# A Mamba block with a memory-routed FFN on one core: the warm-up units replaced by a prologue written out per engine

## What is computed

```
xs  = pixel_shuffle(layernorm_over_channels(x), 2)     # 128 channels, 48 x 48 tokens
seq = concat(global_token, xs as a sequence)           # 2305 tokens for each of 4 images
u, z = split(seq @ in_proj_w.T)                        # 256 inner channels each
u   = silu(causal depthwise conv of 4 taps over u + conv_b)
dt, B, C = split(u @ x_proj_w.T)                       # ranks 8, 16, 16
dt  = softplus(dt @ dt_proj_w.T + dt_proj_b)
h_t = exp(dt_t * A) * h_(t-1) + (dt_t * u_t) * B_t     # 16 states per channel, along the tokens
y   = (sum over states of h_t * C_t + u * D) * silu(z)
x   = x + pixel_unshuffle(y @ out_proj_w.T)
x   = x + ffn(layernorm(x))                            # a routed mix of memory tokens overwrites 128 tokens
```

## Time and profile before

| | us |
|---|---|
| median of three runs | 1269.06 (1267.61 to 1270.39) |
| the profiled execution | 1268.71 |
| its span | 1266.9 |
| busy: POOL, DVE, PE, ACT | 1107.5, 1100.3, 1084.2, 875.3 |

### The profile page before, as it was taken

One profiled execution on the slowest core, in us unless ns is written; L12 is line 12 of the kernel. 1 busy time (PEld: TensorE's weight loads), 2 busy tenths in 40 slices (PEclk: granted clock), 3 DMA queues, 4 the chain that ended last, 5 costly groups with the idle time before them and its releaser, 6 DMA issues.

```text
span 1266.9 us, 13315 instructions
## 1 busy us (share of the span) xinstructions
PE 1084.2 (86%) x3786; PEld 629.6 (50%) x3786; DVE 1100.3 (87%) x1269; ACT 875.3 (69%) x1628; POOL 1107.5 (87%) x753
## 2 busy tenths in 40 slices
PE   6669988888998998888998888899898889979887
PEld 4335545554554554545555544555455445545444
DVE  1299999999989999999899999899999999998672
ACT  2577776776767767767768768767767767667552
POOL 4189899999898999998999999998999999987662
PEclk8699999999999999999999999999999999989799
DMA  6221231322222212212212222222212213223461
GB/s 164 77 77 63 95 100 59 106 90 70 100 71 93 102 58 106 102 58 106 100 59 106 84 76 91 92 83 81 102 62 103 97 62 111 93 77 120 145 209 37
DMA packets 64539, 116.80 MB, mean 92 GB/s; under 512 B 34218, under 2 KB 47954, under 8 KB 64466
## 3 DMA queue, kind: packets, MB, share of 16 engines
q1 hardware_dynamic: 64466, 115.96, 27.1%
HBM read 108.47 MB, written 7.47 MB: 92 GB/s over the span
## 4 chain that ended last, share of the span: by engine, by line
PE 32%; ACT 24%; POOL 16%; DVE 15%; issue 12%; POOLq 0%; DMA 0%; DVEq 0%; SPq 0%; ACTq 0%
PE Yp L738 12%; DVE SCAN L1002 11%; POOL SCAN L427 7%; ACT DA L504 6%; PE PP L889 6%; POOL SCAN L439 3%; DVE SCAN L966 3%; PE PP L871 3%; PE PP L854 2%; PE PP L821 2%; PE PP L767 2%; ACT GATES L610 2%; ACT GATES L601 2%; ACT GATES L604 2%; ACT GATES L608 2%
## 5 line engine op out<-in xcount | busy, mean ns | idle before, releaser
L1002 DVE TENSOR_TENSOR_SCAN SCAN<-DA,CAR,SCAN 128x384 f32<-128x384 f32 x768 | 728.1, 997 | 52.8 <-ACT DA L504 33.2
L427 POOL TENSOR_TENSOR SCAN<-SCAN,CS 128x768 f32<-128x768 f32 x384 | 692.2, 1820 | 47.7 <-DVE SCAN L1002 43.4
L738 PE MATMUL Yp<-SCAN,IDENT 128*128 128x384 f32 x1536 | 589.3, 510 | 64.2 <-POOL SCAN L427 56.0
L504 ACT ACTIVATE DA<-UDT,A 128x384 f32<-128x384 f32 x768 | 431.7, 577 | 260.7 <-DVE SCAN L1002 257.7
L738 PEld LDWEIGHTS Yp<-SCAN,IDENT 128*128 128x128 f32 x1536 | 288.4, 197 | 262.2 <-POOL SCAN L427 102.5
L966 DVE TENSOR_TENSOR SCAN<-UDT,BB 128x768 f32<-128x768 f32 x288 | 268.0, 931 | 8.3 <-PE BB L720 8.2
L439 POOL TENSOR_TENSOR SCAN<-UDT,BS 128x768 f32<-128x768 f32 x96 | 175.0, 1823 | 0.0
L889 PE MATMUL PP<-XN,WT 128*128 128x384 f32 x384 | 140.5, 501 | 5.0 <-ACT GZ L635 5.0
L889 PEld LDWEIGHTS PP<-XN,WT 128*128 128x128 f32 x384 | 72.8, 194 | 64.3 <-issue 20.8
L720 PE MATMUL BB<-PT,SEL 96*128 96x384 bf16 x288 | 97.5, 339 | 3.0 <-DVE SCAN L966 3.0
L455 POOL TENSOR_TENSOR UDT<-UDT 128x768 f32<-128x768 f32 x24 | 43.6, 1815 | 49.2 <-DVE UDT L1083 49.2
(11 more groups left out here) (172 smaller groups left out, 1160.2 us busy)
## 6 DMA issues: line engine op xcount, KB each, us to landing
CS<-bc_rows SPq DMA_DIRECT2D x96, 768.0 KB, 4.0
BS<-bc_rows SPq DMA_DIRECT2D x24, 768.0 KB, 6.0
out<-XN SPq DMA_DIRECT2D x32, 192.0 KB, 2.4
X<-in_x SPq DMA_DIRECT2D x24, 192.0 KB, 3.5
X<-in_L_ffn_memory_tokens SPq DMA_DIRECT2D x16, 256.0 KB, 3.1
XN<-in_L_ffn_memory_tokens SPq DMA_DIRECT2D x16, 256.0 KB, 3.1
bc_rows<-XDT SPq DMA_DIRECT2D x24, 48.0 KB, 1.5
X<-in_L_ffn_memory_router SPq DMA_DIRECT2D x1, 512.0 KB, 3.7
```

The source lines that it names most:

```text
L427: pool.tensor_tensor(M[:, n1 % MRING], HB[:, n1 % HRING], over_halves(CS[:, n1 % CRING]), ALU.mult).then_inc(m_ready, 1)
L504: act.activation(DA[:, h, 0:T], DT[:, par, h], ACT.Exp, scale=A[:, h, n:n + 1])\
L738: last = pe.matmul(Yp[:, h, 0:T], IDENT[:, :], M[:, n3 % MRING, h], start=n3 == 0, stop=n3 == NS - 1)
L1002: dve.tensor_tensor_scan(HB[:, s % HRING, h], DA[:, h, 0:T], HB[:, s % HRING, h], CAR[:, ds(J * NS * HALVES + s * HALVES + h, 1)], ALU.mul ...
```

## The change

The three warm-up units go, and each engine gets a prologue() that is written out in straight lines; the loop starts at unit 0. In the prologue:

- SEL is cleared and filled at GpSimd's start, ahead of its wait for the weights, and no longer between the norm of unit 1 and the gate of unit 0.
- The transposed weights go to DA, not to PP; the projection of unit 0 goes to Yp's second bank (XQ), the global token's results to Yp's first bank (ST0), the mean and variance of units 1 and 2 to BB's two banks. Only the conv halves use PP, and DA holds the step-size projection.
- Unit 0 is convolved right after the weights, ahead of the norm of unit 1.
- The gate of unit 0 runs in halves: exp, clamp, Ln, exp and product of half 0 go while half 1 is convolved, and each half of the projection follows its product.
- XDT is copied ahead of PART, and the step-size projection comes ahead of the remainders. Abs is taken in halves.
- The Relu and the affine step (L595, L615) of unit 0 go; VectorE does all three products of the softplus, and dt u, which GpSimd did.
- The global token's small steps lie between the large ones; its last part (VectorE) comes after dt u.
- Unit 2's variance and the second half of unit 1's convolution come between the first and the second spread of B. ScalarE no longer waits for the starting states ahead of the first decays.

In the loop only the semaphore counts of Relu and the affine step change (by one, since unit 0 no longer gives them).

```diff
-            unit(-3, 1, main=False, front=False, back=False, conv=False)
-            if before_conv:
-                before_conv()
-            unit(-2, 0, main=False, front=False, back=False)
-            if before_front:
-                before_front()
-            unit(-1, 1, main=False, back=False)
...
 @block.gpsimd
+            pool.memset(SEL[:, :, :], 0.0).then_inc(zeroed, 1)
+            for part in range(PARTS):
+                pool.wait_ge(zeroed, 3 + part)
+                pool.affine_select(out=SEL[:, :, :], in_=SEL[:, :, :], compare_op=ALU.not_equal, fill=1.0,
+                                   base=-part * BC, pattern=[[-1, NS], [0, P]], channel_multiplier=1)\
+                    .then_inc(zeroed if part < PARTS - 1 else sel_ready, 1)
             pool.wait_ge(w_loaded, 16 * N_WLOADS)
...
+            normalize(0)
+            for h in range(HALVES):
+                pool.wait_ge(gate_exp, h + 1)
+                pool.tensor_scalar(SG[:, h], SG[:, h], EXP_LIMIT, 0.0, ALU.min, ALU.max)\
+                    .then_inc(clamped if h else gate_clamped, 1)
+            normalize(1)
+            normalize(2)
...
 @block.tensor
+            def prologue():
+                mean(0, STAT)
+                variance(0, STAT)
+                pe.wait_ge(ident_ready, 1)
+                pe.wait_ge(set_dve, 1)
+                for h in range(HALVES):
+                    for k in range(TAPS):
+                        last = pe.transpose(Yp[:, h, k * P:(k + 1) * P], WSC[:, h * TAPS + k], IDENT[:, :])
...
+                pe.wait_ge(set_act, 3)
+                pe.wait_ge(xn_ready, 1)
+                conv_half(0, 0)
+                conv_half(0, 1)
+                pe.wait_ge(set_act, 4)
+                pe.wait_ge(half_u, 1)
+                pe.matmul(XQ[0:XROWS, :], XPT[:, 0], U[:, 0, 0], start=True, stop=False)
...
+                mean(1, BB[:, 0, 0:TOK])
+                pe.wait_ge(u_ready, 1)
+                pe.matmul(XQ[0:XROWS, :], XPT[:, 1], U[:, 0, 1], start=False, stop=True).then_inc(xp_ready, 1)
+                pe.wait_ge(xdt_ready, 1)
+                for h in range(HALVES):
+                    pe.matmul(DA[:, h, 0:T], DTW[DTROW:XROWS + 1, h], XDT[DTROW:XROWS + 1, :],
+                              start=True, stop=True, tile_position=(DTROW, 0)).then_inc(dtp_ready if h else half_dt, 1)
+                variance(1, BB[:, 0, 0:TOK])
...
+                mean(2, BB[:, 1, 0:TOK])
...
+                pe.wait_ge(xn_ready, 2)
+                conv_half(1, 0)
             def first_main():
                 pe.wait_ge(parts_ready, 1)
                 pe.wait_ge(sel_ready, 1)
+                pe.wait_ge(ln_done, 2)
                 spread_b(0, 0, 0)
+                variance(2, BB[:, 1, 0:TOK])
+                conv_half(1, 1)
+                pe.wait_ge(ln_done, 3)
                 spread_b(0, 0, 1)
...
 @block.scalar
...
+                act.wait_ge(conv_ready, 2)
+                act.activation(SG[:, 1], PP[:, 1, 0:T], ACT.Exp, bias=NCB[:, 1:2], scale=-1.0).then_inc(gate_exp, 1)
+                act.wait_ge(clamped, 1)
+                act.activation(SG[:, 1], SG[:, 1], ACT.Ln, bias=1.0).then_inc(sg_chain, 2)
+                act.wait_ge(sg_chain, 2)
+                act.activation(SG[:, 1], SG[:, 1], ACT.Exp, scale=-1.0).then_inc(sg_ready, 1)
...
+                square(1)
+                act.wait_ge(xp_ready, 1)
+                act.activation(XDT[XROW0:XROWS, :], XQ[XROW0:XROWS, :], ACT.Copy).then_inc(xdt_ready, 1)
+                act.activation(PART[:, :], XQ[0:DTROW, :], ACT.Copy).then_inc(hi_ready, 1)
...
             def first_main():
                 act.wait_ge(dt_ready, 1)
-                act.wait_ge(car_saved, 4 * BATCH)
...
 @block.vector
+            def prologue():
+                center(0, STAT)
+                dve.wait_ge(w_loaded, 16 * N_WLOADS)
...
+                dve.wait_ge(gate_ready, 1)
+                dve.scalar_tensor_tensor(out=U[:, 0, 0], in0=PP[:, 0, 0:T], scalar=CB_[:, 0:1], in1=SG[:, 0],
+                                         op0=ALU.add, op1=ALU.mult).then_inc(half_u, 1)
...
+                dve.wait_ge(m1_done, 2)
+                dve.scalar_tensor_tensor(out=DT[:, 0], in0=DA[:, :, 0:T], scalar=0.0, in1=SE[:, :, :],
+                                         op0=ALU.max, op1=ALU.subtract).then_inc(dt_ready, 1)
+                dve.wait_ge(dt_ready, 1)
+                dve.tensor_tensor(DTU[:, 0], DT[:, 0], U[:, 0], ALU.mult).then_inc(dtu_ready, 1)
```

More of the change, by code:

```diff
@@ L401, in _, with normalize @@
                 pool.tensor_copy(XN[:, b * SLOT + HIST - 1:b * SLOT + HIST], TKC).then_inc(const_ready, 1)
-            def selectors():
-                pool.memset(SEL[:, :, :], 0.0).then_inc(zeroed, 1)
-                for part in range(PARTS):
-                    pool.wait_ge(zeroed, 3 + part)
-                    pool.affine_select(out=SEL[:, :, :], in_=SEL[:, :, :], compare_op=ALU.not_equal, fill=1.0,
-                                       base=-part * BC, pattern=[[-1, NS], [0, P]], channel_multiplier=1)\
-                        .then_inc(zeroed if part < PARTS - 1 else sel_ready, 1)
+            def normalize(g):
+                pool.wait_ge(rstd_ready, g + 1)
+                for r1 in range(2):
+                    pool.tensor_tensor(seq_rows(unit_seq(g), r1), by_row_parity(XC[:, :, :], r1),
+                                       by_row_parity(over_q(RSTD[:, :]), r1), ALU.mult).then_inc(xn_part, 1)
+                pool.wait_ge(xn_part, 2 * (g + 1))
+                pool.tensor_copy(XN[:, ds((g + BATCH) * SLOT, HIST)],
+                                 XN[:, ds(g * SLOT + T, HIST)]).then_inc(xn_ready, 1)
             def step(J, par, s, main, front, back, prev, conv, norm):
@@ L460, in step @@
                 if norm and s == 15:
[L462 to L470 removed]
+                    normalize(g)
+            normalize(0)
[5 more added lines that the diff above has]
+            normalize(2)
+            run_units(pool, step)
         @block.scalar
@@ L915, in step, with mean, variance @@
                     last.then_inc(dtp_ready, 1)
+            def mean(g, stat):
+                pe.wait_ge(x_first[g], 16)
+                for q in range(Q):
+                    last = pe.matmul(stat, MEANW[:, :], unit_x(g)[:, q], start=q == 0, stop=q == Q - 1)
+                last.then_inc(mean_ready, 1)
+            def variance(g, stat):
+                pe.wait_ge(sq_ready, g + 1)
+                for q in range(Q):
+                    last = pe.matmul(stat, MEANW[:, :], SQ[:, q], start=q == 0, stop=q == Q - 1)
+                last.then_inc(var_ready, 1)
@@ L932, in _ @@
             last.then_inc(set_dve, 1)
-            def weights():
-                dve.wait_ge(w_loaded, 16 * N_WLOADS)
-                dve.wait_ge(ident_ready, 1)
-                for h in range(HALVES):
-                    dve.tensor_scalar(DD[:, h], IDENT[:, :], DV[:, h:h + 1], None, ALU.mult)
-                dve.memset(LESS[:, :, :], 0.0).then_inc(less_set, 1)
-                dve.wait_ge(less_set, 1)
-                for part in range(1, PARTS):
-                    rows = slice(part * BC, (part + 1) * BC)
-                    for step in range(part):
-                        last = dve.tensor_scalar(LESS[rows, step], IDENT[rows, 0:DTROW], -1.0, None, ALU.mult)
-                last.then_inc(less_set, 1)
             X0v = X[:, 0:BATCH * T].rearrange("p (b q t) -> p q b t", b=BATCH, q=Q)[:, :, :, 0]
@@ L1087, in first_main @@
                 drive(0, 0, 0, 0)
-            run_units(dve, step, before_conv=weights, first_main=first_main)
+            prologue()
+            run_units(dve, step, first_main=first_main)
 _NAMES = ["x", "L0_conv_global_token", "L0_conv_in_proj_w", "L0_conv_conv_w", "L0_conv_conv_b",
```

300 lines of the change are left out of this document (180 added, 120 removed).

## The result

| | before | after |
|---|---|---|
| median of the runs beside each other | 1269.72 (1267.61 to 1270.60) | 1251.12 (1250.23 to 1255.59) |
| the profiled execution, its span | 1268.71, 1266.9 | 1250.23, 1248.5 |
| first scan starts | 64.47 | 45.72 |
| from the first scan to the end of the span | 1202.4 | 1202.8 |

The ratio of after to before is 0.9861, with a 95% interval from 0.9840 to 0.9881. The forecast was 1253.0 in a range from 1246 to 1261.

The account below looks back on a forecast made before the run. Bound: a 64.5 us start-up of engines waiting for each other, then a loop filled by VectorE, GpSimd and TensorE. 7.2 + 3.1 + 2.5 + 4.2 + 4.2 - 5.0 = 16.2; median 1269.06 less 16 gives 1253.0 us, range 1246 to 1261.

Parts of the forecast that it names:

- SEL at GpSimd's start: Opening: VectorE's eight conv-weight scalings take turns with GpSimd's selects, so unit 0's centring starts 5.0 us later, at 12.1.
- rival 1: Opening: selects do not hold up the weight scalings; first scan at 43.3, time 1248 us; chance 0.22.
- The convolution's start: Unit 0, TensorE: with the weights in DA the convolution can follow the last transpose, 7.2 us less.
- The convolution's clock: Unit 0's convolution takes 5.2 us at full clock, 3.1 less than before, with 10.2 as the other end.
- rival 2: Prologue: TensorE's clock stays low, 7.5 us less gain, time 1260.5 us; chance 0.21.
- The gate: Unit 0, convolution's end to second product's end: in halves 2.8 us instead of 5.3, 2.5 less.
- The projection: Unit 0, second product's end to end of XDT's copy: 1.7 us instead of 5.9, 4.2 less.
- From Abs to the first scan: Last stretch of the start-up: 17.3 us, taken between 16.8 and 18.5, against 17.25 before, so no gain.
- Moving SEL off the chain is worth 0.8: Before unit 0's gate clamp: selects and clearing take 8.2 us, but moving them gains 0.8, the convolution being late right behind.
- At no cost: Prologue: B and C rows arrive in time, decays go under the wait for starting states, changed counts cost nothing.
- Rival 3: Before the first scan: the B rows or a mis-ordered wait give back 16 us, time 1269; chance 0.04.
- Rival 4: Loop: a mean clock near 0.88 costs 0.8 us per unit, 17 us in all, time 1270 to 1274; chance 0.03.

Follow-up runs that it names:

- e5: Changed kernel with unit 0's gate in one piece (both exps, one clamp, one Ln, one exp, then both products): 1258.88 us, ratio 0.9914 to the kernel before.
- e9: Changed kernel with the edits of e1, e7 and e8 together: 1245.42 us, ratio 0.9807 to the kernel before.
- e1: Changed kernel with SEL's first select behind GpSimd's token copies, the other two behind unit 0's norm product: 1247.06 us, ratio 0.9820 to the kernel before.
- e3: Kernel before with only SEL's clearing and selects moved to GpSimd's start: 1271.73 us, ratio 1.0016 to the kernel before.
- e4: Changed kernel with unit 1's norm put back ahead of unit 0's convolution on every engine, still in the new banks: 1258.32 us, ratio 0.9904 to the kernel before.
- r3: Changed kernel run again as it is, in the third group: 1251.11 us, ratio 0.9858 to the kernel before.
- r0: Changed kernel run again as it is, in the first group: 1252.20 us, ratio 0.9860 to the kernel before.
- r2: Repeat of e1, selects in GpSimd's gaps of the changed kernel, in the third group: 1248.09 us, ratio 0.9829 to the kernel before.
- e8: e1 with VectorE's first product with B placed behind dt u, inside the token's chain: 1248.78 us, ratio 0.9839 to the kernel before.
- e7: Changed kernel with three extra float32 matmuls, results unread, ahead of TensorE's waits for XPT, u and XDT: 1249.91 us, ratio 0.9842 to the kernel before.
- e2: Kernel before with only the selects for SEL moved one stage earlier, ahead of unit 1's norm: 1269.12 us, ratio 0.9992 to the kernel before.

## Why the forecast was right, step by step

**The whole.** The forecast said that what the first scan gains, the end gains. 18.75 us at the first scan and 18.4 at the end: right. The 1202 us behind it held within 0.4. In the other kernels they lay between 1202.1 (e5) and 1208.3 (e9), so this holds to a few microseconds for a single execution, and the coincidence of 0.4 is partly luck. The experiments undid three parts of the change, one at a time: the place of the selects, the order of unit 1's norm and the halves of the gate. What the rest is worth (the projection behind its halves, the step-size projection ahead of the remainders, the softplus on VectorE) is read from the timelines alone.

**SEL at GpSimd's start.** Forecast 5.0 us for the centring, by turns. Measured 4.12 (7.07 to 11.19). The two engines do take turns, but the eight were through sooner, at 11.27 and not 12.1: with three held up out of eight, one went before the first select and two passed for each select, the one held up and a short one behind it, so that one was left over at the end, not four or five. L1010 was the right row to choose, and e1 and e3 show that the selects are the cause and that rival 1 is wrong. The trace agrees with the page "SBUF — State Buffer" of the Trainium skill, section Who interferes with whom, and now for a select too: 2039 ns at the longest where 279 is the median without one.

**The convolution's start.** Forecast 7.2 us for the banks. Putting unit 1's norm back in e4 takes about 5 of them; the rest is the time in which TensorE waited for PP to be emptied (2.11 us idle ahead of L849), which no run put back. The last transpose (L978) ends at 17.35 and L959's record begins at 17.18, so nothing lies between them. The start was 1.9 us earlier than forecast: 0.9 from the centring, 0.2 from that overlap, and 0.9 between centring and the last transpose, 6.16 us (11.19 to 17.35) against 7.02 before (7.07 to 14.09 in the earlier trace rows), since TensorE's clock rose earlier among the transposes. In r3, where it rose 2 us later than in the first profile, the same stretch took 7.0 again and the start was 17.96, so this 0.9 is luck of the execution. The forecast had left what the clock may give back in the range.

**The convolution's clock.** Forecast 5.2 against 10.2. Measured 5.33 in the first profile, r0, r3, e1, r2, e8 and e9. But e4, e5 and e7 took 6.6 to 7.2, since there the clock rose only within it. So the choice was right as the likeliest, and rival 2 was a live case for a part of it. Its bound of 10.2 leaves out the tail that 5.2 has in it; it should have been 10.5, and no profile came near it.

**The gate.** 3.04 for 2.8: the half clamp was mis-sized at 0.45 and took 0.51, the Ln, the second exp and the product took 0.02 to 0.05 more each, and the handovers 0.3 for 0.2. The gain is 2.3 us, from 5.3, and the halves are not all of it. e5 shows 4.5 for the undivided gate at that place, so halving is worth 1.5. With only the selects moved (e2) the same stretch of the kernel before takes 4.6 (29.91 to 34.55), so 0.7 is the clamp that no longer waits for them, and 0.1 is left for the order around it.

**The projection.** 1.52 for 1.7. ScalarE was in square(1) as said, but the projection's own end (26.49) was only 0.1 before square's (26.56), so that it was not about 1.0 late but in time.

**The step size.** 2.13 for 2.1.

**From Abs to the first scan.** 16.52 for 17.3, and 14.95 in r3. Three VectorE operations at 0.91 are 2.7, not the 2.9 of the sum, which they happened to take (38.77 to 41.72). The sum's form was right: VectorE's list ended last (L1219, 43.64 + 0.25) and TensorE's second spread (43.38 + 0.33) just ahead of it, though the clock had fallen. Its size was not. At the full clock ScalarE's list from Abs to the last of the softplus took 8.0 us (from 29.97 in r3 to 37.96, where L1192 starts, which waits for the last of them), not 9.6: the rows of such a view overlap, and I had added them up whole with handovers on top. In the first profile the wait of 1.53 at L718 filled the gap, and so the forecast looked better than it was. The whole error at the first scan, 48.3 - 45.72 = 2.6 us, is 1.9 for the convolution's start and 0.8 for this part, less 0.2 for the steps in between, and 0.1 of rounding.

**Moving SEL off the chain is worth 0.8.** e2 gained 0.7 in the median, which can't be told from nothing, and in its profile 0.66 at the clamp and 0.4 at the first scan, counted from the convolution's end.

**At no cost.** Right for the rows of B and C: the DMA share is 0.88 from 30 to 38 us, 0.06 from 38 to 40 and 0.00 behind, ahead of the scan. That the x tiles of the kernel before were all but through by 26 us does not follow from the share of 0.85 that the forecast cites; they were, as the share from 26 to 28 us is 0.00.

**The rivals.** Rival 1 fell with L1047's longest record, and with e1 and e3. Rival 2 (7.5 us less gain) did not come, but its mechanism is real: a fall of the clock behind the convolution took 1.6 us in one execution of the same program and nothing in another. Rival 3: no wait was mis-ordered. Rival 4: from the first scan on the mean clock was 0.95 (0.96 before), and the stretch cost the same as before.

## What to carry to other kernels

Before setup work is moved to an engine's empty stretch, look at what the other engine of the pair VectorE and GpSimd does there: eight instructions of 0.28 us took 6.9 beside three selects of 2.1, and with the selects in later gaps they took 1.66 again. A piece on the chain of waits is worth only what lies between it and the next thing that is late (8.2 us on it, 0.7 in the time), so name that next thing before you price the piece. And where an order leaves TensorE idle ahead of a chain of small matmuls, put that chain at the slow clock into the range: the gate in one piece cost 6.7 us, where its own chain explains 1.5 and the order around it had been priced at 2 more.

## What the runs showed of the hardware that I had not expected

- TensorE's granted clock in the start-up differs between executions of one program. The changed kernel had it at 0.50 from 30 to 38 us in one profile and at 1.00 up to 44 in another, although TensorE was busy for all of the 2 us from 28 to 30 in both; e1 and r2 lost it at about 26, e9 at 29. The moment at which it first rises moves too (in unit 0's convolution in e4, e5 and e7, ahead of it in the other seven profiles of kernels made from the changed one). I have found no rule for either, and that stays open; the chip may have a part in it. It makes the spread of single runs of the changed kernel, 3.1 to 5.4 us in its three sets, plausible, but that link was not tested.
- The window view reads 1.00 in the first microseconds, while the variance L954 takes 2.02 us at 12.41, as L854 did before, and 1.13 for unit 1 in r3 at the full clock. For the opening, durations tell the clock, not the window's figure.
- On a half tile (384 wide) instead of a full one (768) GpSimd's clamp takes 0.51 for 0.82, ScalarE's exp 0.52 for 0.84, VectorE's product 0.62 for half of 1.14: so halving costs 0.05 to 0.1 per piece.
